# Relative attention: the order of TensorE's blocks in the loop over windows

## What is computed

```python
q_head = (hidden @ Wq.T + bq) in 16 heads of 8;  k_head, v_head in the same way
score_1 = jnp.einsum('bhqd,bhkd->bhqk', q_head, k_head)
score_2 = jnp.einsum('qmd,qkd->qmk', q_resh, rel_k[clip(q - k, -128, 128) + 128])
attn = jax.nn.softmax((score_1 + score_2) / sqrt(8), axis=-1)
weight_1 = jnp.einsum('bhqk,bhkd->bhqd', attn, v_head)
weight_2 = jnp.einsum('qmk,qkd->qmd', se, rel_v[clip(q - k, -128, 128) + 128])
out = (weight_1 + weight_2) @ Wo.T + bo
```

## Time and profile before

| what | us |
|---|---|
| median of 3 runs | 1481.24 |
| lowest and highest | 1480.29, 1485.09 |
| the profiled execution | 1486.69 |
| its span in the trace | 1484.8 |
| PE busy, share of the span | 1243.1, 84% |
| DVE busy, share | 1003.1, 68% |
| ACT busy, share | 728.2, 49% |

### The profile page before, as it was taken

The page is one execution under the profiler, slowest core; times in us unless marked ns, Lnnn a source line. Parts: engine busy times, 40 slices in busy tenths (PEclk is TensorE's granted clock), DMA queues, the critical chain, the costliest instruction groups (busy, mean ns, idle before and its releaser), DMA issues.

```text
span 1484.8 us, 46393 instructions
## 1 busy us (share of the span) xinstructions
PE 1243.1 (84%) x19317; PEld 781.3 (53%) x19317; DVE 1003.1 (68%) x2562; ACT 728.2 (49%) x1814; POOL 232.4 (16%) x200
## 2 busy tenths in 40 slices
PE   6879898797689899898994889988998899889775
PEld 4343434295366666566662346634673466346554
DVE  4567576545677777777762678677868786878542
ACT  1313141443266667665661329532954295329543
POOL 2011121142030130131002030004000400030044
PEclk8889798888899999999996899989999999999988
DMA  9800000022340010100003100000000000060021
GB/s 313 311 17 1 17 1 8 8 59 79 120 158 4 18 33 4 30 21 11 11 4 89 45 1 2 4 1 15 2 4 1 15 2 2 1 158 3 2 78 48
DMA packets 61024, 63.21 MB, mean 43 GB/s; under 512 B 27756, under 2 KB 51569, under 8 KB 59664
## 3 DMA queue, kind: packets, MB, share of 16 engines
q1 hardware_dynamic: 55184, 51.68, 11.6%
q0 software_dynamic: 2752, 5.29, 1.1%
q10 hardware_dynamic: 2880, 3.28, 0.6%
HBM read 32.58 MB, written 28.55 MB: 41 GB/s over the span
## 4 chain that ended last, share of the span: by engine, by line
PE 57%; DVE 19%; ACT 12%; issue 7%; POOL 2%; DMA 2%; SPq 1%; ACTq 1%; POOLq 0%; DVEq 0%
PE ps L1195 5%; PE ps L1205 5%; DVE arena L633 4%; PE ps L1616 4%; PE ps L1221 3%; PE ps L505 3%; ACT arena L1707 3%; DVE arena L1771 3%; PE ps L531 3%; PE ps L1245 3%; DVE arena L1781 2%; PE ps L274 2%; PE ps L1671 2%; ACT arena L1717 2%; ACT arena L1315 2%
## 5 line engine op out<-in xcount | busy, mean ns | idle before, releaser
L1357 DVE TENSOR_REDUCE nmax<-ps 128x1 f32<-128x512 f32 x256 | 166.5, 682 | 68.8 <-PE ps L1205 68.6
L1707 ACT ACTIVATE arena<-ps,arena 128x512 f32<-128x512 f32 (+3 forms) x256 | 134.6, 539 | 74.4 <-DVE arena L1771 71.3
L1315 ACT ACTIVATE arena<-ps,nmax 128x512 f32<-128x512 f32 x172 | 118.7, 693 | 75.4 <-DVE nmax L1357 74.5
L1771 DVE TENSOR_REDUCE arena<-ps 128x1 f32<-128x512 f32 (+3 forms) x256 | 115.6, 484 | 14.4 <-PE ps L1631 12.8
L633 DVE TENSOR_REDUCE arena<-ps 128x8 f32<-128x1232 f32 x64 | 89.4, 1437 | 29.6 <-PE ps L493 28.6
L1365 DVE COPY arena<-ps 128x512 f32<-128x512 f32 x128 | 87.2, 681 | 22.4 <-PE ps L1221 22.3
L1781 DVE TENSOR_SCALAR arena<-arena 128x512 f32<-128x512 f32 (+3 forms) x256 | 92.0, 391 | 5.7
L274 PE MATMUL ps<-identb 128*128 128x512 bf16 x241 | 75.5, 468 | 23.0 <-DVE var L318 10.7
L1717 ACT COPY arena<-ps 128x512 f32<-128x512 f32 x160 | 85.8, 596 | 12.5 <-PE ps L1646 12.5
L1646 PE MATMUL ps<-sqc,arena 64*128 64x64 f32 x1280 | 67.4, 235 | 24.3 <-ACT arena L1717 11.0
L1662 PE MATMUL ps<-arena 128*64 128x128 f32 x1280 | 87.5, 279 | 0.0
(11 more groups left out here) (358 smaller groups left out, 2557.8 us busy)
## 6 DMA issues: line engine op xcount, KB each, us to landing
xs_d<-onehot SPq DMA_DIRECT2D x3, 2704.0 KB, 28.6
gs_d<-kmask SPq DMA_DIRECT2D x8, 645.0 KB, 10.0
cw<-in_cw SPq DMA_DIRECT2D x2, 2048.0 KB, 12.0
rv<-in_rv SPq DMA_DIRECT2D x2, 1536.0 KB, 17.3
late<-in_gw SPq DMA_DIRECT2D x3, 1024.0 KB, 10.9
arena<-gs_d SPq DMA_DIRECT2D x23, 129.0 KB, 2.0
xs_d<-onehot SPq DMA_DIRECT2D x1, 2288.0 KB, 20.9
onehot<-q_s SPq DMA_DIRECT2D x96, 8.0 KB
```

The lines of the kernel that those rows point to most:

```text
L1315: nc.scalar.activation(PB[k % 6], ps[:, k % 5, :], ACT.Exp, bias=nmax[:, u:u + 1], accum_out=rsum[:, b % 2, u:u + 1]).then_inc(SD["exp"], 1)
L1357: nc.vector.tensor_reduce(nmax[:, k % NU:k % NU + 1], ps[:, k % 5, :], AX.X, ALU.max, negate=True)\
L1707: ins = nc.scalar.activation(TF["p%d" % (n % 2)][:, h * S + c0:h * S + c1], ps[:, FSB[n % 2][h], c0:c1], ACT.Exp, bias=TF["nmax"][:, k8:k8 ...
L1771: ins = nc.vector.tensor_reduce(TF["nmax"][:, k8:k8 + 1], ps[:, FSB[n % 2][h], c0:c1], AX.X, ALU.max, negate=True)
```

## The change

In `pe_D` the four relative matmuls of a window become a function of their own, `relative(Q)`. PE's order for one window is now `scores(Q + 1)` (query-key products alone), `flips(Q, 0)`, `relative(Q + 1)`, `flips(Q, 1)`, `values(Q - 1)`; where a batch ends, `spread_own` stands ahead of `flips(Q, 1)` and `spread_other` ahead of `values(Q - 1)`, as before. On ACT `copy(2Q)` stands ahead of `exp(4Q + 4)`, on DVE ahead of `top(4Q + 4)` and `top(4Q + 5)`. Instructions, semaphores, counts that are waited for, and buffers stay.

```diff
--- before.py
+++ after.py
@@ -1196,6 +1196,9 @@
                                          ALL[b % 2][GW * r:GW * (r + 1), j % 2, j // 2 * NW + w, :, :],
                                          KT[b % 2][GW * r:GW * (r + 1), :], start=True, stop=False, skip_group_check=True,
                                          tile_position=(GW * r, GW * c))
+
+            def relative(Q):
+                b, w = Q // NW, Q % NW
                 for par in range(2):
                     for z in range(2):
                         j = 2 * par + z
@@ -1288,18 +1291,20 @@
                                      start=True, stop=True, skip_group_check=True).then_inc(SD["r"], 1)
 
             scores(0)
+            relative(0)
             for Q in range(NQ):
                 if Q + 1 < NQ:
                     scores(Q + 1)
                 done = Q // NW - 1 if Q % NW == 1 and Q > 1 else None
                 flips(Q, 0)
+                if Q + 1 < NQ:
+                    relative(Q + 1)
                 if done is not None:
                     spread_own(done)
-                elif Q >= 1:
-                    values(Q - 1)
                 flips(Q, 1)
                 if done is not None:
                     spread_other(done)
+                if Q >= 1:
                     values(Q - 1)
             values(NQ - 1)
             spread_own(B - 1)
@@ -1335,10 +1340,9 @@
                 exp(k)
             for Q in range(NQ):
                 more = Q + 1 < NQ
+                copy(2 * Q)
                 if more:
                     exp(4 * Q + 4)
-                copy(2 * Q)
-                if more:
                     exp(4 * Q + 5)
                     exp(4 * Q + 6)
                 copy(2 * Q + 1)
```

## The result

| what | before | after |
|---|---|---|
| median, us | 1482.7 (4 runs) | 1536.4 (4 runs) |
| lowest and highest, us | 1480.3, 1485.1 | 1534.2, 1541.4 |
| the profiled execution, us | 1486.7 | 1534.2 |

The changed kernel is slower by 3.67% (ratio 1.0367, 95% interval 1.0335 to 1.0399), that is by 50 to 59 us. 1525 had been forecast, in a range of 1505 to 1545. The two profiled executions stand 47.5 us apart, against a sum of +44 made for them; the medians are 53.7 apart, because the profiled execution of before was slower than the four runs of its kernel and the one of after the fastest of its own.

A forecast was written before the change was run, and what follows sets the result against it. A loop through three engines (relative products, top, exp, query-key products) was taken to set the 5.21 us period. +49 for late picks and -5 for gaps gave +44 on 1481.2: 1525 us, range 1505 to 1545.

The forecast's parts named there:

- The bound: Relative-attention stage: a loop of relative products, top, exp and query-key products through three engines sets the 5.21 us period.
- T before R, copies first: First transposes ahead of relative products, copies ahead of exp and tops: loop takes 5.33 us against 5.21, 0.12 worse.
- The decisive step: VectorE, even iterations: later values delay pick and the copy behind it; next transposes wait 1.21 us, the pair takes +1.41.
- Other positions: Across a batch's windows, extra per pair is about 1.42 us in the first half, 1.75 in the second, mean 1.58.
- the term of 49: Relative-attention stage: 31 picks inside the loop at 1.58 us each make it 49 us slower.
- The gaps: TensorE's 18.3 us of "issue" before relative values and transposes, without a cause: new slack absorbs some, -5 us.
- The faster case: TensorE's blocks decide: fewer tile-shape changes (3 us) and waits for exp gone (10.3 us) give 1468 us; chance 0.03.
- That nothing would change: The new wait before the transposes only takes the place of TensorE's idle time: 1481 us; chance 0.03.
- The clock case: Each of 31 new TensorE pauses brings one relative block at lowered clock, 19 us more: 1544 us; chance 0.09.
- The gap case: TensorE's pauses before the transposes absorb all 18 us of "issue" gaps, slower by only 31: 1512 us; chance 0.09.
- the alternation: Profile sign: time between successive query-key blocks alternates, about 5.3 to 5.6 us, then 6.5 to 7.1.
- the wait at L1224: Profile sign at the transposes (formerly L1221): wait for a copy, 1.2 us or more in most of 31 places, 35 to 50 in all.

The follow-up runs named there:

- The split wait: Kernel before, with the query-key products' one wait for exp split in four, each unit waiting only for its own bank's exp: 1477.5 us, ratio 0.998.
- the merged values: Kernel before, with own values as 16 matmuls of 128 columns per window instead of 32 of 64: 1459.3 us; with the wait for exp also split, 1446.1.

## Why the prediction was right

**The bound.** R, top, exp and S in a circle set the pace, with PE close behind. The split wait bears both out, though not in a time clear of noise: S's waits fell from 14.4 to 2.6 us, and the stage became 3.4 us shorter; with the merged values as well, from 17.4 to 1.7, and 9.8 shorter.

**T before R, copies first.** 5.33 was worked out for the short iteration, 5.35 was measured. The 0.12 over 5.21 is there.

**The decisive step.** "The first T of the next iteration waits for this copy" came out to 0.01 us in the pair shown, and 29 of 30 windows have such a wait. That it acts through VectorE's queue is shown by the move of pick and add alone: with TensorE's order as changed, the wait is gone and all but some 5 us with it.

**Other positions.** The growth with R and W can't be checked one by one under the standstills. (By the code half of a window's relative matmuls are 8 columns wider than the widths given, 144 to 384; by the rows that is 0.01 to 0.03 us a block.) The stage as a whole grew by 51.3 us. Less the growth of the pauses inside blocks, 4.6, that is 46.7, against the term of 49.

**The gaps.** This term had the wrong sign. The forecast let 5 us of standstills vanish in the new slack; the pauses inside blocks grew instead, from 16.4 to 21.0 us. With 49 and +5 the sum would be 54, near the 51.3 of the stage. The row itself ("issue", 18.3 us) was read as time without a cause, and it has one: code that has not yet arrived, at fixed places of PE's program. More waiting elsewhere doesn't absorb it as a rule: the pauses in blocks are 9.4 us with the copies moved and 26.4 with the values moved, and both kernels make PE wait longer than before. Why the one has few of them and the other many stays open.

**The rivals.** The faster case needed the copy to end 6.25 us after S; in the pair shown it ended at 446.23 and the S of its window had started at 438.70, so at 7.53 (7.46 forecast). The change of tile shape, of which the new order has one less per window, was worth 0.05 us by the rows and can't be seen in the result. That nothing would change is ruled out by the interval (50 to 59 us). The clock case did not occur: the mean granted clock of the stage is 0.96, 0.97 before. The gap case went the other way.

**The number.** 54 us by the medians were 10 more than the 44 forecast. The range reached that high because of the clock case, which did not occur; that it also covered the gaps' wrong sign was luck.

**Where the profile was to show it.** Right: the alternation (5.35 and 6.53 in the pair), pick's 32 waits, and the size of the wait at L1224, 34.7 us under "issue" and 3.1 under ACT's copy, where 35 to 50 were forecast. Wrong: the name of that wait, and S's waits for exp, which were to hold or shrink and rose from 14.4 to 20.7 us. The stage grew by 51.3 us where 44 were said, and what follows it was not as long as before but 4.1 shorter.

## What to carry to other kernels

Before a producer is moved later in its engine's program, look in the consumer engine's queue at what stands behind the instruction that waits for it: here the values' reader had time, the copy queued behind it had none, and two instructions moved behind that copy gave nearly all of it back. Where an engine stands still inside a block with no wait in the program, compare the ends of the pauses with the packets of the instruction queue, and their places with a packet's worth of the engine's own instructions (256 here); fewer and wider matmuls of the same duration were worth 25 us. And a wait for a whole group of buffers can be split into one wait per buffer.

## What was not expected of the hardware

Halving the number of own-value matmuls while doubling their columns (64 to 128) left their block as long as it was (0.90 and 0.92 us), and yet took 1.6 to 2.5% off the kernel. PE's pauses inside blocks end about 1.4 us after the end of a packet of the instruction queue (127 of 141 in the nine kernels that have nine pauses or more), and all but one of them stand at the same place of a stretch of 256 of PE's instructions. A wait for a semaphore can be shown as "issue" when it is 1.13 us long and its releaser is plain from the timeline. The stage after the changed one was 4 us shorter without a change of its own, and the other kernels took 694 to 706 us for it, without an edit there either: a few us of difference between two profiled executions say nothing about an edit.
